# Gate products of a GRU layer: x as high and low f32r parts instead of f32

## What is computed

```python
h = jnp.concatenate([x[row], x[col]], axis=-1)
msgs = jax.nn.silu(h @ W1.T + b1) @ W2.T + b2
agg = jax.ops.segment_sum(msgs, row, num_segments=n_nodes)
agg = agg / (cnt + 1e-08)
gi = agg @ w_ih.T + b_ih
gh = x @ w_hh.T + b_hh
r = jax.nn.sigmoid(i_r + h_r)
z = jax.nn.sigmoid(i_z + h_z)
n = jnp.tanh(i_n + r * h_n)
x_new = (1.0 - z) * n + z * x
...
return gamma * (x_new - mu) / jnp.sqrt(var + 1e-05) + beta
...
x = _layernorm(x + _L0_gnn_ref(...), axis=-1)
```

## Time and profile before

| | us |
|---|---|
| median of 3 runs | 2585.26 |
| the profiled execution | 2583.86 |
| its span | 2582.2 |
| setup, to about | 48 |
| edge stage, to about | 1035 |
| a turn of the node stage (1200 us, 156 turns) | 7.69 |

### The profile page before, as it was taken

The page is one execution under the profiler, slowest core; times in us unless marked ns, Lnnn a source line. Parts: engine busy times, 40 slices in busy tenths (PEclk is TensorE's granted clock), DMA queues, the critical chain, the costliest instruction groups (busy, mean ns, idle before and its releaser), DMA issues.

```text
span 2582.2 us, 45968 instructions
## 1 busy us (share of the span) xinstructions
PE 2476.6 (96%) x11010; PEld 1786.1 (69%) x11010; DVE 2173.4 (84%) x6131; ACT 1275.0 (49%) x2168; POOL 1397.8 (54%) x1377
## 2 busy tenths in 40 slices
PE   5999999999999997799999999999999999999996
PEld 3888888888888885466666666666666666666663
DVE  5666666666666665599999999999999999999998
ACT  2444444444444443355555555555555555555554
POOL 4444444444444440466666666666666666666663
PEclk9999999999999999899999999999999999999998
DMA  3555555555555555456666666666666666666662
GB/s 104 213 213 213 213 213 212 212 214 215 215 215 214 213 214 194 161 191 211 205 206 207 207 212 204 205 202 202 201 206 206 204 201 205 209 204 205 202 201 100
DMA packets 190976, 519.44 MB, mean 201 GB/s; under 512 B 50914, under 2 KB 52322, under 8 KB 190948
## 3 DMA queue, kind: packets, MB, share of 16 engines
q1 hardware_dynamic: 115684, 312.66, 34.7%
q0 software_dynamic: 75264, 206.47, 25.3%
HBM read 467.55 MB, written 206.32 MB: 261 GB/s over the span
## 4 chain that ended last, share of the span: by engine, by line
PE 41%; DVE 27%; issue 19%; POOL 9%; DVEq 2%; POOLq 1%; DMA 1%; ACT 0%; SPq 0%; ACTq 0%
PE banks L811 38%; DVE st L744 7%; POOL xb L367 5%; PE banks L823 3%; POOL mg L311 3%; DVE diff L728 3%; DVE xn L739 3%; DVE uu L773 3%; DVE ag L750 2%; DVE oh L707 2%; DVE rhn L716 2%; DVE tg L762 2%; POOL rows_now L348 1%; DVE ve L756 1%; DVEq L706 0%
## 5 line engine op out<-in xcount | busy, mean ns | idle before, releaser
L811 PE MATMUL banks<-whh,xts 128*128 128x512 f32 (+1 forms) x3136 | 1138.8, 485 | 0.0
L811 PEld LDWEIGHTS banks<-whh,xts 128*128 128x128 f32 x3136 | 594.5, 190 | 340.7 <-issue 281.8
L311 POOL DMA_INDIRECT mg<-messages,rows_now x392 | 497.6, 1269 | 379.2 <-PE banks L811 311.0
L311 POOL DMA_INDIRECT xsrc<-in_x,src_now x196 | 186.6, 952 | 497.6 <-PE banks L823 492.9
L479 ACT ACTIVATE nt<-npre 128x512 f32<-128x512 f32 x196 | 123.9, 632 | 642.7 <-DVE npre L722 642.7
L570 DVE TENSOR_TENSOR msg<-banks,msg 128x512 fp32r<-128x512 f32 (+1 forms) x392 | 201.8, 556 | 207.9 <-ACT msg L434 204.2
L811 PE MATMUL banks<-mg,oh 128*128 128x512 f32 (+1 forms) x1568 | 328.9, 352 | 47.2 <-DVE oh L707 31.5
L434 ACT ACTIVATE msg<-banks 128x512 fp32r<-128x512 f32 (+1 forms) x392 | 192.2, 490 | 312.1 <-PE banks L811 305.9
L811 PEld LDWEIGHTS banks<-mg,oh 128*128 128x128 f32 x1568 | 258.4, 189 | 124.3 <-issue 50.6
L473 ACT ACTIVATE banks<-banks,rcount 128x768 f32<-128x768 f32 x392 | 322.9, 860 | 42.0 <-PE banks L811 42.0
L811 PE MATMUL banks<-bias_n,ones 128*128 128x512 f32 x392 | 312.3, 797 | 0.0
(11 more groups left out here) (111 smaller groups left out, 4308.5 us busy)
## 6 DMA issues: line engine op xcount, KB each, us to landing
messages<-msg SPq DMA_DIRECT2D x196, 772.0 KB
xts<-in_xt SPq DMA_DIRECT2D x196, 256.0 KB
xs<-in_x SPq DMA_DIRECT2D x196, 256.0 KB
out_y<-yy SPq DMA_DIRECT2D x196, 256.0 KB
mg<-messages,rows_now POOLq DMA_INDIRECT x392
xsrc<-in_x,src_now POOLq DMA_INDIRECT x196
xdst<-in_x,dst_now POOLq DMA_INDIRECT x196
wih<-in_wiht SPq DMA_DIRECT2D x1, 768.0 KB
```

What stands on the lines that cost most here:

```text
L311: nc.gpsimd.indirect_dma_start(out=dst_tile, out_offset=None, in_=rows, in_offset=bass.IndirectOffsetOnAxis(ap=table, axis=0), bounds_chec ...
L811: return nc.tensor.matmul(out_, lhsT, rhs, start=start, stop=stop, skip_group_check=skip)
```

## The change

`whh` is split in the setup into `wxh` (ScalarE) and `wxl` (VectorE). In each turn ScalarE copies `xts` into the f32r tile `xh` (`x_hi`, lag 2, ahead of `gates0`), and GpSimd subtracts it from `xts` into `xl` (`x_lo`, lag 2, at the head of its turn). TensorE makes three f32r products where it made one f32 product. Transposed x is loaded for q+4 and x for q+1, in steps of their own; transposed x now waits for `xl`, x as before for `diff` and `xb`.

```diff
-        whh = sb("whh", [P, KC, G3])
+        wxh, wxl = sb("wxh", [P, KC, G3], f32r), sb("wxl", [P, KC, G3], f32r)
...
+        xh, xl = sb("xh", [P, QU, 2 * D], f32r), sb("xl", [P, QU, 2 * D], f32r)
...
             def load_x(q, u):
-                need(sp, S["n_mm"], q - QU + 1)
+                need(sp, S["n_xl"], q - QU + 1)
                 sp.dma_start(xts[:, u, :], xt[bass.ds(q * P, P), :]).then_inc(got_xt[u], 16)
+
+            def load_rows(q, u):
                 need(sp, S["n_diff"], q - QU + 1)
                 need(sp, S["n_xb"], q - QU + 1)
                 sp.dma_start(xs[:, u, :], x_pairs[bass.ds(q * P, P), :]).then_inc(got_x[u], 16)
...
-            node_turns(sp, ((load_x, 3), (store_y, -8)), first=-3, last=8)
+            node_turns(sp, ((load_x, 4), (load_rows, 1), (store_y, -8)), first=-4, last=8)
...
+                def x_lo(q, u):
+                    pool.wait_ge(S["n_xh"], q + 1)
+                    need(pool, S["n_mm"], q - QU + 1)
+                    nc.gpsimd.tensor_tensor(out=xl[:, u, :], in0=xts[:, u, :], in1=xh[:, u, :].bitcast(f32),
+                                            op=ALU.subtract).then_inc(S["n_xl"], 1)
...
-                node_turns(pool, ((gather_rows, 4), (inv_std1, -2), (inv_std2, -5), (add_beta, -2)), first=-4, last=5)
+                node_turns(pool, ((x_lo, 2), (gather_rows, 4), (inv_std1, -2), (inv_std2, -5), (add_beta, -2)), first=-4, last=5)
...
+            nc.scalar.activation(wxh[:, :, :], whh[:, :, :], ACT.Copy).then_inc(wx_hi, 1)
+            act.wait_ge(wx_lo, 1)
             act.wait_ge(rb_ready, RB_PARTS)
             edge_slots(act, edge_slot, first=QUAD)
+
+            def x_hi(q, u):
+                act.wait_ge(got_xt[u], 16 * (nth(q, u) + 1))
+                need(act, S["n_mm"], q - QU + 1)
+                nc.scalar.activation(xh[:, u, :], xts[:, u, :], ACT.Copy).then_inc(S["n_xh"], 1)
...
-            node_turns(act, ((tanh, -1), (last_norm, -7), (gates0, 0), (mean_scale, 1), (gates1, 0)), first=-1, last=8)
+            node_turns(act, ((tanh, -1), (last_norm, -7), (x_hi, 2), (gates0, 0), (mean_scale, 1), (gates1, 0)), first=-2, last=8)
...
+            dve.wait_ge(wx_hi, 1)
+            nc.vector.tensor_tensor(wxl[:, :, :], whh[:, :, :], wxh[:, :, :].bitcast(f32), ALU.subtract)\
+                .then_inc(wx_lo, 1)
...
             def node_products(q, u, h):
-                pe.wait_ge(got_xt[u], 16 * (nth(q, u) + 1))
+                pe.wait_ge(S["n_xl"], q + 1)
                 pe.wait_ge(S[f"n_sc{h}"], q + 1)
                 o = pn[u % 2]
                 mm(o[:, h, 0, :], ones[:, :], bias_rz[:, :], False, False, True)
                 for c in range(KC):
-                    last = mm(o[:, h, 0, :], xts[:, u, (2 * h + c) * P:(2 * h + c + 1) * P], whh[:, c, 0:2 * D],
-                              False, c == KC - 1, True)
+                    hi, lo = (t[:, u, (2 * h + c) * P:(2 * h + c + 1) * P] for t in (xh, xl))
+                    mm(o[:, h, 0, :], hi, wxh[:, c, 0:2 * D], False, False, True)
+                    mm(o[:, h, 0, :], hi, wxl[:, c, 0:2 * D], False, False, True)
+                    last = mm(o[:, h, 0, :], lo, wxh[:, c, 0:2 * D], False, c == KC - 1, True)
```

More of the change, by code:

```diff
@@ L120, in gnn_layer @@
         b2b = sb("b2b", [P, KC, P], until=setup)
-        wih = sb("wih", [P, KC, G3], until=setup)
+        wih, whh = (sb(n, [P, KC, G3], until=setup) for n in ("wih", "whh"))
         brow = sb("brow", [1, 6 * D], until=setup)
@@ L150, in gnn_layer @@
         idx_ready, w1_hi, w1_ready = sem("idx_ready"), sem("w1_hi"), sem("w1_ready")
+        wx_hi, wx_lo = sem("wx_hi"), sem("wx_lo")
         b2_ready, wc_mm, wc_hi, wc_lo = sem("b2_ready"), sem("wc_mm"), sem("wc_hi"), sem("wc_lo")
@@ L170, in gnn_layer @@
         names = ("n_oh n_sg0 n_sg1 n_sc0 n_sc1 n_g0 n_g1 n_mm n_rz0 n_rz1 n_rhn n_npre n_tanh n_diff n_xb n_zd n_xn"
-                 " n_s1 n_a1 n_v1 n_r1 n_tg n_u n_s2 n_a2 n_v2 n_r2 n_nmr n_y").split()
+                 " n_xh n_xl n_s1 n_a1 n_v1 n_r1 n_tg n_u n_s2 n_a2 n_v2 n_r2 n_nmr n_y").split()
         S = {n: sem(n) for n in names}
@@ L951, in node_products @@
                 for c in range(KC):
-                    last = mm(o[:, h, 1, D:2 * D], xts[:, u, (2 * h + c) * P:(2 * h + c + 1) * P], whh[:, c, 2 * D:G3],
-                              False, c == KC - 1, True)
+                    hi, lo = (t[:, u, (2 * h + c) * P:(2 * h + c + 1) * P] for t in (xh, xl))
+                    mm(o[:, h, 1, D:2 * D], hi, wxh[:, c, 2 * D:G3], False, False, True)
+                    mm(o[:, h, 1, D:2 * D], hi, wxl[:, c, 2 * D:G3], False, False, True)
+                    last = mm(o[:, h, 1, D:2 * D], lo, wxh[:, c, 2 * D:G3], False, c == KC - 1, True)
                 return last
```

## The result

The changed kernel took 3029.95 us (median, 3028.05 to 3039.43), the kernel before 2585.95: a ratio of 1.1725, 95% interval 1.1699 to 1.175. It is 17% slower. The direction was forecast; the size, 2768 with a range to 2870, was not.

A forecast was written before the change was run, and what follows sets the result against it. VectorE was taken to set the node-stage turn of 7.69 us. A turn of 8.6, 0.91 more, over 196 turns gave 178 us; with 4.6 of setup on 2583.86, plus 1.4 to the median, 2768 us, range 2650 to 2870.

The forecast's parts named there:

- GpSimd's own load: Node stage, GpSimd's queue: 7.8 us in one turn, 6.8 in the next, 7.3 on average against 8.6; doesn't lead yet.
- What bounds the kernel before: Node stage: VectorE sets the 7.69 us turn, `uu` standing still beside `xb` for 0.38; TensorE needs 7.18.
- TensorE's part: Node-stage products: three f32r passes for four, a turn's need 6.6 us instead of 7.2, worth nothing since VectorE lies above.
- ScalarE's copy: Node stage, ahead of `gates0`: one 128x512 copy a turn, 0.53 to 0.6 us, hidden.
- The lock: Node stage: GpSimd's subtraction holds VectorE's `diff` or `zd`; 1.3 us taken, turn of 8.6, 178 us in all.
- the third rival: Node stage: port no matter for TENSOR_TENSOR, subtraction runs freely beside `diff`, `zd`, `xn`; 2515 to 2590 us, chance 0.11.
- the sign that I named: VectorE in the node stage: `diff` or `zd` with a mean of over 1.1 us, `xl` beside it, if forecast right.
- The second rival: Node stage: GpSimd leads, its queue needing over 8.8 us, VectorE or TensorE waiting for `oh` or `xb`; 2885 us, chance 0.12.
- Setup: Setup: two instructions over 1536 columns delay the twelve bias steps from 40.50 to 45.1; TensorE waits, 4.6 us.
- Loads of x for q+1: Node stage: x issued about 17 us before `diff` reads it, 256 KB in 1.3 us at 205 GB/s; costs nothing.

## Why the prediction was wrong

The forecast of GpSimd's own load left out what waits behind the new subtraction: VectorE's wait for late gathers, 1.41 us a turn, which the prediction put at nothing. The parts in their order:

*What bounds the kernel before*: right that VectorE leads and that `uu` stands still beside `xb`. The loss was mis-sized, 0.38 for 0.46, because I took the group's busy total, in which the overlap of neighbours counts once, and subtracted 312 x 478 ns, in which it counts twice. And VectorE led by less than I thought: TensorE needs 7.5, so of the 0.46 only about 0.2 can be had, as the run with the small `xb` showed.

*TensorE's part*: right in kind. It waits for `npre` 275.9 / 120 = 2.3 us a turn (forecast 2) at a busy share of 77% (80). Its granted clock was 0.86 on average. After an idle time of 5.3 us, up to 2004.01, it was granted 0.50, the lower of its two levels (1.2 GHz), and products of 512 columns started 0.43 us apart; from about 2008.2 on, with TensorE busy since 2004.01, it was granted 1.00 and they started 0.23 apart (columns as in the busy row at the top):

```profile
2006.70:2007.90 1.20, 1.20 (x4) 1.00 (x4) 1.20 (x1) 1.20 (x2) 1.03 (x2) 0.50 0.00 0
2008.30:2010.30 2.00, 2.00 (x13) 1.78 (x12) 2.00 (x6) 0.60 (x1) 1.70 (x2) 1.00 0.26 28
```

In this kernel that cost next to nothing, VectorE waited 3.5 us for TensorE in 120 turns.

*ScalarE's copy*: right, 0.61 us, hidden.

*The lock*: right in mechanism; right in its total, but by luck. TENSOR_TENSOR is held like SCALAR_TENSOR_TENSOR, which disposes of the third rival: `zd` took 1.65 beside `xl` from 2006.11. The total was forecast at 1.3 a turn in place of 0.38 and measured at 1.30 in place of 0.46. Its parts are others. I had `xl` hold `diff` or `zd` in every turn, at 1.05 or more; it held them in 61 of 120 turns, 0.44 us a turn, and the sign that I named, a mean of over 1.1 us, was not there (`diff` 0.84, `zd` 0.96). In its place `nmr` lost 0.34 and `tg` 0.25, on which I had put nothing, and I took `oh` for free ground, which it is not. With the gathers no longer late but `xl` full on GpSimd, the locks came to 1.61 to 2.61.

*GpSimd's own load*: **the step that failed.** I asked whether GpSimd's queue was full, found 7.3 us against 8.6, and left it there. GpSimd was indeed only 62% busy. But I had written down that the subtraction waits for this turn's `npre`, and did not follow what is queued behind it to its readers. The gathers had been a turn early because GpSimd ran ahead; they were put into the sum as if they still were. In place of that VectorE waits 1.41 us a turn, 276 us over 196 turns: 1.23 of it for gathered rows, 0.15 for `rs`, which stands in the same queue. So VectorE is busy for 84% of the stretch and not for 98. The two runs that take the gathers out from behind the wait by GpSimd's list alone bring 133 and 230 us back; the rest is taken by larger locks. The second rival has VectorE waiting for `oh`, but from a queue that is too long, which is not what happened.

*Setup*: right, 4.3 us for 4.6. TensorE takes up the edge stage at 51.93 instead of 47.67.

```profile
43.10 1.76 DVE L619 TENSOR_TENSOR wxl<-whh,wxh 128x1536 fp32r<-128x1536 f32 x1 [9.02 <-ACT wxh L465]
...
51.93 0.49 PE L831 MATMUL banks<-ohb,upto 128*128 128x392 f16 x1 [12.12 <-issue]
```

*Loads of x for q+1*: right that nobody waits for them. They land in 3.6 us, not in the 1.3 that the bandwidth alone gave.

So 2585 + 4 + 196 x (0.84 + 1.41 + 0.06 that the sum leaves open) = 3042, against 3030 measured. Without the 276 us of waiting it would be 2766, and the forecast was 2768: the term left out is about the whole miss. That the others meet the forecast so closely is luck, as said of the lock.

## What to carry to other kernels

When a wait is put at the head of an engine's turn, redo the lead time of everything queued behind it, above all of DMAs that this engine issues: an engine that is 54% busy may still be early by design, and the reader of a gather that lands 6.4 us after its issue notices when it isn't. Before work is given to an engine with time to spare, ask which instructions of the leading engine it will stand beside; here a subtraction of 1.3 us on the spare engine cost 209 us more in all than the same one of 0.59 us on the full engine. And a lock that can't be avoided can be placed: two waits and a new place in GpSimd's list, which put `xb` beside instructions that it can't hold, made the old kernel 1.6% faster.

## What the runs showed of the hardware

- A GpSimd TENSOR_TENSOR of 128x512 with both inputs in SBUF holds VectorE's `uu`, `tg`, `nmr`, `diff`, `zd` and `xn`. Beside a GpSimd instruction of this kind TENSOR_SCALAR instructions are held too that read one SBUF tile: `ve` 128x4 took 1.24 us in all (0.17 normal), `oh` 128x128 took 1.31 (0.34 normal) beside `xl` in the run with the subtraction for q+1. `rhn` and `npre` with an operand in PSUM and the statistics of `xn` and `uu` kept their lengths in every run (0.66 to 0.69, 0.69, 0.41 to 0.42). The Trainium skill (SBUF — State Buffer, "Who interferes with whom") says that copies, casts and tensor_scalar can take the shared port too, in their two-port modes; that `ve` and `oh` were held agrees, but no run shows in which mode they ran.
- Counted back from its end by its normal length, a held instruction was let go about 1.1 us after the printed start of `xb` or `xl` (1.01 to 1.22 in nearly all cases; 1.30 for `zd` beside an `xl` that itself took 1.45). The stop may last a little longer: `ve` and `nmr`, the shortest, end only 0.03 us behind the end of `xb`, as they would if their first 0.1 to 0.15 us had been done before the stop. The runs don't tell the two readings apart, so the 1.09 of the prediction doesn't show the lock to end before the GpSimd instruction does.
- The start in the trace is not the start of the lock. When `xb` follows `rs` at once, VectorE instructions that began before the printed start of `xb` were held until about 1.1 us after it: `uu` at 2002.56 beside `xb` at 2003.13, and an `oh` that began 0.99 us ahead (1486.31 and 1487.30). So one instruction can lose 2.0 us. Not all are held so: in the kernel before, 76 `tg` lay wholly inside an `rs` with `xb` right behind it, and all kept their 0.47 us. Why the stop can begin so early stays open.
